# A vision tower on one NeuronCore: the first two convolution groups in chunks and in six banks, dummy products at the start, a cast moved to POOL

## What is computed

```
pe  = conv_general_dilated(pixel_values, conv_w, (14, 14), 'VALID')   # 588 inputs per patch -> 256 channels
red = mean of pe over each 3x3 window
win = the nine positions of each window
q   = ln(red) @ la_wq ;  kv = ln(win) @ la_wkv
...
```

## Time and profile before

| | |
|---|---|
| timed runs | 209.2, 209.75, 210.35 us; median 209.75 us |
| profiled execution | span 207.1 us from the first to the last instruction; its own time outside the span is not recorded |
| PE busy | 193.5 us (93%), 1134 products |
| DVE, ACT, POOL busy | 139.5, 108.1, 78.6 us |
| DMA | 32.90 MB, 159 GB/s over the span, near 400 GB/s in the first 25 us |

### The profile page before, as it was taken

One profiled execution on the slowest core, in us unless ns is written; L12 is line 12 of the kernel. 1 busy time (PEld: TensorE's weight loads), 2 busy tenths in 40 slices (PEclk: granted clock), 3 DMA queues, 4 the chain that ended last, 5 costly groups with the idle time before them and its releaser, 6 DMA issues.

```text
span 207.1 us, 3427 instructions
## 1 busy us (share of the span) xinstructions
PE 193.5 (93%) x1134; PEld 169.3 (82%) x1134; DVE 139.5 (67%) x337; ACT 108.1 (52%) x234; POOL 78.6 (38%) x107
## 2 busy tenths in 40 slices
PE   1899999999999997999998999999999999999991
PEld 1899899988898875867777799988788888888881
DVE  1565976285999997945698847757586767766411
ACT  4666294464525554544742452163687767677321
POOL 4017266265555040159435534683042221112220
PEclk9999999999999999999999969999999999999998
DMA  6999995000293000000002910125999887933003
GB/s 204 359 393 397 356 331 174 0 3 0 60 418 135 0 0 3 0 0 2 3 0 41 410 59 2 51 102 129 386 413 418 298 305 314 309 97 106 0 0 76
DMA packets 10189, 32.90 MB, mean 159 GB/s; under 512 B 1190, under 2 KB 5628, under 8 KB 8508
## 3 DMA queue, kind: packets, MB, share of 16 engines
q1 hardware_dynamic: 8120, 29.53, 39.3%
q10 hardware_dynamic: 1764, 2.37, 3.3%
q0 software_dynamic: 288, 0.79, 1.1%
HBM read 30.05 MB, written 2.64 MB: 158 GB/s over the span
## 4 chain that ended last, share of the span: by engine, by line
PE 75%; DVE 14%; ACT 3%; DMA 3%; issue 3%; ACTq 0%; DVEq 0%
PE bank L1062 15%; PE bank L584 10%; PE bank L1082 9%; PE bank L661 6%; PE bank L990 4%; PE bank L1095 4%; PE bank L599 3%; DMA raw<-xa 3%; PE bank L1000 3%; PE bank L1071 2%; PE bank L608 2%; DVE stats L1697 2%; PE bank L885 2%; PE bank L894 1%; DVE kv_rows L1751 1%
## 5 line engine op out<-in xcount | busy, mean ns | idle before, releaser
L1062 PE MATMUL bank<-split 128*128 128x512 f32 x132 | 33.2, 400 | 0.1
L1628 POOL TENSOR_SCALAR split<-token_row,window 128x384 fp32r<-128x384 f32 x11 | 15.5, 1413 | 45.7 <-PE bank L1095 45.7
L584 PE MATMUL bank<-split 128*128 128x256 f32 (+1 forms) x225 | 28.3, 285 | 0.0
L1062 PEld LDWEIGHTS bank<-split 128*128 128x128 f32 x132 | 24.0, 188 | 5.1 <-DVE split L2159 0.3
L584 PEld LDWEIGHTS bank<-split 128*128 128x128 f32 (+1 forms) x225 | 27.5, 191 | 0.2
L661 PE MATMUL bank<-split 128*128 128x512 f32 x108 | 26.5, 397 | 0.0
L1532 POOL TENSOR_TENSOR rstd<-veps,mhalf 128x1 f32<-128x1 f32 (+2 forms) x17 | 14.2, 835 | 29.8 <-DVE veps L1704 29.6
L661 PEld LDWEIGHTS bank<-split 128*128 128x128 f32 x108 | 19.8, 188 | 3.9
L1982 DVE TENSOR_TENSOR split<-raw,split 128x512 fp32r<-128x512 f32 x28 | 18.1, 684 | 5.9 <-ACT split L1376 5.8
L1376 ACT CAST split<-raw 128x512 fp32r<-128x512 f32 x28 | 16.7, 620 | 2.0 <-DMA raw<-ffn_w 2.0
L1552 POOL TENSOR_TENSOR window<-window,pe_rows 128x256 f32<-128x256 f32 x14 | 14.4, 1032 | 8.3 <-ACT pe_rows L1157 7.8
(11 more groups left out here) (281 smaller groups left out, 401.8 us busy)
## 6 DMA issues: line engine op xcount, KB each, us to landing
raw<-ffn_w SPq DMA_DIRECT2D x7, 1024.0 KB, 6.9
kv_rows<-ffn_w SPq DMA_DIRECT2D x4, 1024.0 KB, 5.4
raw<-xa SPq DMA_DIRECT2D x5, 768.0 KB
raw<-ffn_w SPq DMA_DIRECT2D x7, 512.0 KB, 7.0
kv_rows<-ffn_w SPq DMA_DIRECT2D x4, 512.0 KB, 5.7
tok<-tok_w SPq DMA_DIRECT2D x1, 1536.0 KB, 12.2
raw<-ffn_w SPq DMA_DIRECT2D x1, 1536.0 KB, 6.7
expert_rows<-zero_row SPq DMA_DIRECT2D x1, 1419.0 KB, 11.9
```

Source lines behind the costliest of these rows:

```text
L584: mm = pe.matmul(bank[b][:, 0:C], xs[0:n, g % 2, px, a:a + P], cws[0:n, pw, k, :], start=(k == 0 and m == 0), stop=(k == len(KCH) - 1 and ...
L1062: mm = pe.matmul(bank[half][:, :], xst[:, s % 2, px, c * P:(c + 1) * P], tile_aws[s % 2][:, piece, pw, :], start=(c == 0 and m == 0), stop ...
L1628: pool.tensor_scalar(back[:, s % 2, :], token_row[:, :], xr[:, s % ROW_RING, ROW_TOKEN:ROW_TOKEN + 1], None, ALU.is_equal).then_inc(back_d ...
```

## The change

- Group 0: patches and weights come chunk by chunk, each with a semaphore of its own. ACT issues the patch chunks 0 to 2 in three transfers; SP issues the weight chunks 0 to 3 singly, patch chunk 3 among them, then the two last chunks.
- POOL casts the weights' high parts; ACT casts patches alone. DVE subtracts the weights before the patches in each chunk.
- Group 1 is also cast and subtracted chunk by chunk, in the second half of the split buffer. Its three tiles get banks 3, 4 and 5 of their own. PE multiplies the high patches of each chunk by both weight parts first, with `value_shift` ahead of chunk 3, and then the low patches of all chunks.
- PE makes eight products of `mean_w` with itself (128x128, plain float32) into bank 7 before anything else.
- `weights_scaled` moves from ACT to DVE. On ACT the three copies of group 0 come ahead of four bias loads, and the three of group 1 behind the cast of group 2. The small load `crow` moves from ACT to SP.
- SP's order becomes: group 1, `tok` first piece, `crow`, group 2, `con`, group 3, group 4, `tok` second piece, group 5, `att`.

```diff
-CONV_BANK = [*range(GT)] + [(i + 1) % 2 for i in range(GT, TILES)]
+EARLY = 2
+CONV_BANK = [*range(EARLY * GT)] + [(i + 1) % 2 for i in range(EARLY * GT, TILES)]
+WARM = 8
...
-            sp.dma_start(cw_raw[:, 0, :], conv_w[0:P, :]).then_inc(cw_in[0], 16)
-            sp.dma_start(cw_raw[:, 1:4, :], conv_w[P:4 * P, :].rearrange("(k p) c -> p k c", p=P)).then_inc(cw_in[1], 16)
-            load_rest(sp, cw_raw[:, 4, :], conv_w[4 * P:KC, :], cw_in[2])
-            load_rest(sp, x_raw[:, 0, 4, :], xb[0], x_in[0])
+            for k in range(len(KCH) - 1):
+                if k == 3:
+                    sp.dma_start(x_raw[:, 0, k, :], xa[0][:, k * GT * P:(k + 1) * GT * P]).then_inc(first_in[k], 16)
+                sp.dma_start(cw_raw[:, k, :], conv_w[k * P:(k + 1) * P, :]).then_inc(cw_in[k], 16)
+            load_rest(sp, x_raw[:, 0, 4, :], xb[0], first_in[4])
+            load_rest(sp, cw_raw[:, 4, :], conv_w[4 * P:KC, :], cw_in[4])
...
+            load_group(1)
+            sp.dma_start(tok[:, 0:TOK_FIRST], tok_w[:, 0:TOK_FIRST]).then_inc(tok_in, 16)
+            sp.dma_start(crow[:, :], rows[1:3, :]).then_inc(con_in, 16)
+            load_group(2)
+            sp.dma_start(con[:, :], consts).then_inc(con_in, 16)
+            load_group(3)
+            load_group(4)
+            sp.dma_start(tok[:, TOK_FIRST:], tok_w[:, TOK_FIRST:]).then_inc(tok_rest_in, 16)
+            load_group(5)
+            sp.dma_start(att[:, :], att_w).then_inc(att_in, 16)
...
+            def warm_up():
+                pe.wait_ge(mean_w_done, 1)
+                for _ in range(WARM):
+                    pe.matmul(bank[7][:, 0:P], mean_w[:, :], mean_w[:, :], start=True, stop=True)
+
+            def early_products(g, k, ms):
+                n = KCH[k][1]
+                for m in ms:
+                    px, pw = PRODUCTS[m]
+                    pe.wait_ge(early_split[g] if px == LO else early_hi[g], k + 1)
+                    if g == 0:
+                        pe.wait_ge(cw_split if pw == LO else cw_hi, k + 1)
+                    for j in range(GT):
+                        a = (k * GT + j) * P
+                        last = k == len(KCH) - 1 and m == 2
+                        mm = pe.matmul(bank[GT * g + j][:, 0:C], xs[0:n, g, px, a:a + P], cws[0:n, pw, k, :],
+                                       start=(k == 0 and m == 0), stop=last)
+                        if last:
+                            mm.then_inc(filled[GT * g + j], 1)
...
+            def second_convs():
+                pe.wait_ge(cw_split, len(KCH))
+                for k in range(len(KCH)):
+                    if k == 3:
+                        value_shift()
+                    early_products(1, k, (0, 1))
+                for k in range(len(KCH)):
+                    early_products(1, k, (2,))
...
+            warm_up()
             first_convs()
-            value_shift()
-            conv_group(1)
+            second_convs()
             weight_mean()
...
+            for k, (_, n) in enumerate(KCH):
+                pool.wait_ge(cw_in[k], 32 if k > 3 else 16)
+                pool.tensor_copy(cws[0:n, HI, k, :], cw_raw[0:n, k, :]).then_inc(cw_hi, 1)
             pool.wait_ge(init_done, 1)
...
             for k, (_, n) in enumerate(KCH):
-                first_patches_lo(k, n)
                 conv_weights_lo(k, n)
-            patches_lo(1)
+                early_patches_lo(0, k, n)
+            for k, (_, n) in enumerate(KCH):
+                early_patches_lo(1, k, n)
+            weights_scaled()
             group_moments(0)
             patches_lo(2)
             weights_centred()
```

More of the change, by code:

```diff
@@ L132 @@
                                                             "loT0", "in0", "in1", "in2"],
-    ["turn0", "turn1", "turn2", "q0", "turn3", "turn4", "turn5", "gs", "ctx0", "mid0"],
-    [f"kv{i}" for i in range(0, TILES, KV_BANKS)] + ["loT1", "gv", "qkv_pool", "ctx1", "mid1"],
-    [f"kv{i}" for i in range(1, TILES, KV_BANKS)] + ["wp2"],
+    ["conv3", "turn0", "turn1", "turn2", "q0", "turn3", "turn4", "turn5", "gs", "ctx0", "mid0"],
+    ["conv4"] + [f"kv{i}" for i in range(0, TILES, KV_BANKS)] + ["loT1", "gv", "qkv_pool", "ctx1", "mid1"],
+    ["conv5"] + [f"kv{i}" for i in range(1, TILES, KV_BANKS)] + ["wp2"],
     ["bv"] + [f"kv{i}" for i in range(2, TILES, KV_BANKS)] + ["wp0"],
@@ L354, in tower_kernel @@
         x_hi, x_split = sem("x_hi"), sem("x_split")
+        early_hi, early_split = ([sem(f"{n}{g}") for g in range(EARLY)] for n in ("early_hi", "early_split"))
         turned_hi = sem("turned_hi")
@@ L359, in tower_kernel @@
         ids_full, gathered, onehot_dve = sem("ids_full"), sem("gathered"), sem("onehot_dve")
-        x_first_in, x_mid_in = sem("x_first_in"), sem("x_mid_in")
+        first_in = [sem(f"first_in{k}") for k in range(len(KCH))]
         x_in = [sem(f"x_in{g}") for g in range(GROUPS)]
-        cw_in = [sem(f"cw_in{n}") for n in range(3)]
+        cw_in = [sem(f"cw_in{k}") for k in range(len(KCH))]
         att_in, con_in = sem("att_in"), sem("con_in")
@@ L586, in conv @@
                 mm.then_inc(filled[b], 1)
-            def first_convs():
[L590 to L602, removed]
+            def warm_up():
[16 more added lines that the diff above has]
+                            mm.then_inc(filled[GT * g + j], 1)
+            def first_convs():
+                for k in range(len(KCH)):
+                    early_products(0, k, (0, 1, 2))
+            def second_convs():
[4 more added lines that the diff above has]
+                    early_products(1, k, (0, 1))
+                for k in range(len(KCH)):
+                    early_products(1, k, (2,))
             def turn(b, name, pieces):
@@ L1149, in _ @@
         def _(act):
-            act.dma_start(x_raw[:, 0, 0, :], xa[0][:, 0:GT * P]).then_inc(x_first_in, 16)
-            act.dma_start(x_raw[:, 0, 1:4, :], xa[0][:, GT * P:].rearrange("p (k n) -> p k n", k=3)).then_inc(x_mid_in, 16)
+            for k in range(3):
+                act.dma_start(x_raw[:, 0, k, :], xa[0][:, k * GT * P:(k + 1) * GT * P]).then_inc(first_in[k], 16)
             def conv_copy(i):
@@ L1163, in patches_hi @@
             def patches_hi(g):
-                if g == 0:
-                    dst = xs[:, 0, HI, :].rearrange("p (k n) -> p k n", k=len(KCH))
+                if g < EARLY:
+                    dst = xs[:, g, HI, :].rearrange("p (k n) -> p k n", k=len(KCH))
                     for k, (_, n) in enumerate(KCH):
[L1168 to L1171, removed]
+                        act.wait_ge(*((x_in[g], 48) if g else (first_in[k], 32 if k > 3 else 16)))
+                        act.copy(dst[0:n, k, :], x_raw[0:n, g, k, :]).then_inc(early_hi[g], 1)
                     return
@@ L1285, in _ @@
             patches_hi(1)
-            act.dma_start(crow[:, :], rows[1:3, :]).then_inc(con_in, 16)
+            conv_copies(0)
             act.dma_start(bias[:, :], biases.broadcast_to([P, BIAS_N])).then_inc(bias_in, 16)
@@ L1833, in conv_weights_lo, with early_patches_lo, weights_scaled @@
                                   ALU.subtract).then_inc(cw_split, 1)
[L1835 removed]
+            def early_patches_lo(g, k, n):
                 cols = slice(k * GT * P, (k + 1) * GT * P)
[L1838 to L1840 removed]
+                dve.wait_ge(early_hi[g], k + 1)
+                dve.tensor_tensor(xs[0:n, g, LO, cols], x_raw[0:n, g, k, :], xs[0:n, g, HI, cols].bitcast(F32),
+                                  ALU.subtract).then_inc(early_split[g], 1)
+            def weights_scaled():
+                wait_full(dve, 6, "bv")
+                for c in range(CC):
+                    cols = slice(2 * c * C, 2 * (c + 1) * C)
+                    ins = dve.tensor_scalar(w_tok("wkv")[:, cols], w_tok("wkv")[:, cols], w_tok("kv_g")[:, c:c + 1], None, ALU.mult)
+                ins.then_inc(wkv_scaled, 1)
             def turned_lo(g):
```

34 lines of the change are left out of this document (6 added, 28 removed).

## The result

The changed kernel takes 208.15 us in the median of 20 executions, the one before 209.6 in 20 beside it: a ratio of 0.991 (95% interval 0.9884 to 0.9935), 1.45 us. The forecast was 2.2. Of 223 timed executions of this study (all but the 20 of the kernel before just named) the mean granted clock is on record, and about 197 us go with a unit of it (one stretch of 3.4 us at the low level lowers the mean by 0.008). Before it is 207.36 (81 executions, from the experiments), after 206.19: a gain of 1.17 (two standard errors 0.28).

The account below looks back on a forecast made before the run. PE was taken as the bound, so conv group 2 starting before 22.44 us is time won. Gained 2.3 by group 1's end, less a 0.1 wait, gives 2.2: 209.75 to 207.55 us, range 206.4 to 209.5 (own range 206.9 to 208.3).

Parts of the forecast that it names:

- Start and first pause: Group 0 on PE: first product at 4.4 us, and the old pause before chunk 1 (0.71 us) gone.
- The dummies: Eight products ahead of group 0: end near 2.8 us, 1.6 us pause follows, worth nothing; rate rises at 8.0 regardless.
- The rival that they free the clock: Dummies raise PE's rate early: group 0 ends at 9.9, gain 2.8 us, 206.95, rest lost to the load; chance 0.20.
- Group 1's load: In at 10.8 us (between 10.2 and 11.3); PE may start group 1 at 11.4, so no wait after group 0's 11.5.
- Group 2 on DVE: Scaling 1.4 us, moments to 17.5, subtraction 2.75 to 20.25; PE, ready at 20.2, waits 0.1 us before conv group 2.
- my late bound: ACT's casts of group 2 were put at 15.4 to 16.5 us, hardly later than DVE's row.
- Signs: Wrong if: short products from first or long until 11, group 2 waiting for DVE, PE idle before group 1, second low-clock stretch.
- Does it carry?: From conv group 2 to the end PE leads and DVE has room, so all moves together and 2.2 us stays.
- `tok`'s second piece: Load behind groups 3 and 4, in at 25.4 to 28 us, used at 30.4; no cost taken, 0.3 at the late end.
- The rise did not stay at 11.2: Rival: PE's rate rises at 11.2 as before, group 0 ends at 12.9; gain 0.85 us, 208.9; chance 0.17.
- DVE did not make the kernel slower: Rival: scaling costs 3.2 us and DVE's subtraction of group 2 ends at 24.2, 1.8 late: 211.55; chance 0.08.
- given back: Rival: a second low-clock stretch like that at 120.40 to 123.90 costs 1.75 us, leaving 0.45: 209.3; chance 0.10.

Follow-up runs that it names:

- the first experiment: The changed kernel without the eight dummy products (WARM from 8 to 0): 207.94 us, ratio 0.9927.
- the second profile: Profile of the unedited changed kernel run again as the last experiment: span 204.0 us; median of those runs 207.69 us, ratio 0.9907.
- the first profile: Profiled execution of the changed kernel from the main measurement, one of its longer ones: span 208.0, time 209.84 us.
- the second experiment: The changed kernel with ACT's four bias loads moved behind the cast of group 2 and the copies of group 1: 207.84 us, ratio 0.9941.
- the eighth and ninth experiments: Eighth: changed kernel without dummies, group 2 cast and subtracted in five chunks, 207.77 us; ninth: the same with key and value weight scaling back on ACT, 207.67 us.

## Why the prediction was right in kind and too large in size

*Start and first pause.* Right. The first product came at 4.52 for 4.4, POOL's first cast took 0.40 as its nearest row did (a later one, beside DVE's subtractions, 0.81), and chunk 1 caused no pause.

*The dummies.* The working was wrong, the worth was right. I had eight products end near 2.8 with a pause of 1.6 behind them, by the price of six transposes; a plain float32 product stands as two records of 0.24 us each, and they ended at 4.76, where the first real one begins. That they just fill the gap is luck. So the rate rose near 7 in one profile and before 5 in the other, not at 8.0; without them, in the first experiment, it rose near 8.5, close to my 8.0. The rival that they free the clock was right on the clock, and right that the rest is lost to the load, but its 206.95 is not reached: without dummies the gain at equal clock is the same, 1.26 against 1.17.

*Group 1's load: the first term that was mis-sized.* Forecast 10.8, measured 11.21 and 11.31. I priced SP's three more issues at 0.36 each; group 1's first issue came at 5.61 instead of 4.02, 1.6 later and not 1.1. Beside that 294 GB/s were moved from 5 to 10 us, where I had put the old rate. So PE starts group 1 at 11.87 to 11.96 instead of 11.4; from there it needs 8.9 us to the third group (11.96 to 20.85), where I had summed 8.8. This is 0.5 of what is missing. That the gain needs the chunked start of group 1 is shown: with the wait for the whole group it is gone. How much of it that start is worth alone is not, since `value_shift` stood behind that wait too.

*Group 2 on DVE: the second.* I had its row end at 20.25, after a subtraction of 2.75 from 17.5 on. In the second profile it ended at 20.2, with the scaling at 1.29 for my 1.4, but by luck: the subtraction began at 17.99, half a microsecond late, and took half a microsecond less, its 76x384 piece 0.55 where my price held the 1.08 of the earlier trace rows. In the first profile it took the 2.75 and ended at 21.56; what was late was its start, at 18.81, behind group 2's load and casts (my late bound was for the casts to be done at 16.5; they were done at 18.8). I had put that load at 4.1 MB moved, at 308 GB/s by 13.4; the rate up to there was 275, and when the load landed, at 16.86, 4.9 MB had been moved in all. Which transfers beside it are to blame is open; by the second experiment it is not the bias loads. So the wait of PE was nothing in one execution and 0.87 in the other, and I had given the load's lateness no weight. That DVE's row and the load are both close to the end is shown by the eighth and ninth experiments: with one wait taken away the other held PE until 21.88, with both taken away there is none.

With 0.5 for group 1's load, that makes up the 1.4 us missing in the first profile (21.62 for 20.2: PE is ready at 20.75 and waits 0.87), and nearly all of the 0.65 in the second (20.85). In the first the lateness of group 1 alone changed nothing, since group 2 came later still. Over many executions the same two terms show: with both waits at group 2 taken away the gain at equal clock is 1.64, and what then still lacks of 2.2 is about the 0.5 of group 1's load.

*Signs.* Two that I had named for being wrong did show: PE idle ahead of group 1 (0.63 and 1.63), and, in the first profile, conv group 2 waiting for DVE's subtraction.

*Does it carry?* Yes, as far as the router: of the 0.82 won at the third group in the first profile 0.56 was there at 118 us (conv group 2 itself had run 0.27 longer), of the 1.59 in the second all. `tok`'s second piece, which I had given 0.3 at worst, delayed nothing: the product that uses it ran at 32.03 (32.58 before).

*The rivals.* The rise did not stay at 11.2. DVE did not make the kernel slower: the scaling cost 1.30, near the low bound, and what ran long beside POOL's additions was the small subtraction, 1.08. The stretch of low clock did come out twice as long in one profiled execution, but over 20 executions the mean clock is 0.990, as in the 81 of the kernel before, so nothing is given back on average; the difference between 1.45 and 1.17 is within the uncertainty.

*A better version?* With both waits at group 2 taken away the gain at equal clock is 0.47 larger than the changed kernel's (two standard errors 0.31, 22 executions against 27). The medians, 207.67 and 207.69, do not tell it from the changed kernel's 207.69 beside them. I cannot settle it with these runs. Also open is what moves the landing of group 1's load between 10.6 and 12.1 us among kernels that issue it alike.

## What to carry to other kernels

Starting a group of products on its first chunk is worth at most the casts and the subtractions that it no longer waits for; the next load then sets the start, so issue counts and packet sizes ahead of it belong in the sum. Speeding up work that ends in a wait wins nothing, and when two waits of one length stand behind each other, take both away before judging either. Where the clock varies from execution to execution, compare times at the same mean clock, or an effect of half a per cent hides behind a stretch of low clock.

## What the runs showed of the hardware

The clock that rises early can fall again at a pause: the granted clock went to 0.50 to 0.56 in the windows shown, which is the level of 1.2 GHz, in or behind pauses of 2.00 us with the dummies alone, of 1.51 with two loads, and of 3.46 with the whole wait. It did not behind 1.30 us with the dummies alone, nor behind 0.63 in the changed kernel or 1.63 in its second profile (the clock stood at 1.00 in the stretches that followed), so the length of the pause alone does not decide here. The Trainium skill, page TensorE: Matmul & The Clock Gate, section "What's actually happening", says that the default state is throttled and that activity releases it; the earlier rise behind the dummies (near 7 us and before 5, against 8.5 without them) agrees.

PE can be busy throughout and still lose the clock: near 120 us it fell at the end of eighteen narrow products (128x8, 2.2 us before, 2.5 after). It does not do so each time: behind the same eighteen it stood at 1.00 in the second profile of the changed kernel. With four wide ones put between them it stood at 1.00 there, and the mean clock was 0.995 or more in all seven executions. At the head the granted clock is written as 1.00 while products take 439 ns, so there the durations and not the clock row tell the level.
